# The first expert loop of a two-layer mixture kernel: results stored from two buffers, weights split by ScalarE and VectorE, loads issued by SyncE

## What is computed

```python
# first mixture: top 2 of 8 experts, width 256 -> 256 -> 256
inter = jnp.einsum('ecd,efd->ecf', binned, w1_stack)
inter = jnp.square(jax.nn.relu(inter))
outb = jnp.einsum('ecf,edf->ecd', inter, w2_stack)
moe_out = zeros.at[sorted_tok].add(outb[sorted_e, local_pos] * sorted_w[:, None])
...
# second mixture: top 2 of 8, width 256 -> 512 -> 256, with biases
h = jax.nn.silu(g) * u          # g = x @ gate_w + gate_b, u = x @ up_w + up_b
expert_out = jnp.einsum('nef,efd->ned', h, down_w) + down_b
y = jnp.einsum('ne,ned->nd', probs, expert_out)
```

## Time and profile before

| | us |
|---|---|
| median of 3 runs | 1300.96 |
| profiled execution, device time | 1300.48 |
| its span | 1298.7 |
| TensorE busy | 1114.3 (86%) |
| VectorE busy | 724.2 (56%) |
| ScalarE busy | 383.7 (30%) |
| GpSimd busy | 376.0 (29%) |

### The profile page before, as it was taken

How to read it: one execution, slowest core, us unless ns; L and a number is a source line. 1 busy time by engine, 2 the same in 40 slices (tenths; PEclk the granted TensorE clock), 3 DMA queues, 4 the chain that set the end, 5 groups by cost and what they waited for, 6 DMA issues and landing times.

```text
span 1298.7 us, 17826 instructions
## 1 busy us (share of the span) xinstructions
PE 1114.3 (86%) x5947; PEld 886.8 (68%) x5947; DVE 724.2 (56%) x1840; ACT 383.7 (30%) x705; POOL 376.0 (29%) x312
## 2 busy tenths in 40 slices
PE   8899899897766657999999967999999649999991
PEld 5467576685556554677887835787878339999990
DVE  5576735757444435465646554445354746666665
ACT  3131221312233224234243333243332123333330
POOL 2423062231435540001111123010101465444710
PEclk9999999999888889999999989999999969999995
DMA  9000051000475734100000000000000586555416
GB/s 327 1 0 34 1 185 28 1 1 5 141 203 161 227 109 137 33 1 1 1 1 1 1 34 34 1 1 1 1 1 1 176 269 186 153 155 168 128 55 210
DMA packets 90851, 102.92 MB, mean 79 GB/s; under 512 B 18336, under 2 KB 75936, under 8 KB 90656
## 3 DMA queue, kind: packets, MB, share of 16 engines
q1 hardware_dynamic: 65920, 59.85, 15.1%
q0 software_dynamic: 20240, 36.72, 9.1%
q10 hardware_dynamic: 4624, 5.51, 1.2%
HBM read 73.31 MB, written 28.74 MB: 79 GB/s over the span
## 4 chain that ended last, share of the span: by engine, by line
PE 50%; issue 18%; DVE 14%; DMA 7%; ACT 4%; POOL 4%; SPq 2%; DVEq 0%; POOLq 0%; ACTq 0%
PE PS L210 12%; PE PS L212 11%; PE PS L211 10%; PE PS L1709 7%; DMA results<-y,place_of 3%; PE PS L1597 2%; POOL routed L843 2%; PE PS L1569 2%; PE PS L1481 1%; PE PS L1681 1%; DMA split<-down_w 1%; POOL rstd L836 1%; DMA places<-routed 1%; PE PS L1475 1%; DVE hs L588 1%
## 5 line engine op out<-in xcount | busy, mean ns | idle before, releaser
L836 POOL TENSOR_TENSOR rstd<-ve,minus_half 128x4 f32<-128x4 f32 x40 | 41.3, 1033 | 350.9 <-DVE ve L1101 210.9
L535 POOL DMA_INDIRECT results<-y,place_of x80 | 78.2, 978 | 184.2 <-DVE y L624 110.5
L1481 PE MATMUL PS<-ones_bf 128*128 128x512 bf16 x393 | 103.7, 410 | 19.1 <-DMA routed<-S,dest 16.0
L210 PE MATMUL PS<-xt,split 128*128 128x256 f32 x312 | 90.2, 289 | 9.2 <-issue 6.1
L211 PE MATMUL PS<-xt,split 128*128 128x256 f32 x312 | 89.0, 285 | 0.0
L212 PE MATMUL PS<-xt,split 128*128 128x256 f32 x312 | 88.9, 285 | 0.0
L1709 PE MATMUL PS<-VP,HB 128*128 128x257 f32 x384 | 85.8, 382 | 0.7 <-DVE VP L1407 0.5
L843 POOL DMA_INDIRECT routed<-S,dest x64 | 66.1, 1033 | 67.1 <-DVE dest L1181 49.3
L1481 PEld LDWEIGHTS PS<-ones_bf 128*128 128x128 bf16 x393 | 39.0, 105 | 66.7 <-issue 34.2
L210 PE MATMUL PS<-split,hs 128*128 128x256 f32 x184 | 59.7, 324 | 25.8 <-DVE hs L588 19.9
L1709 PEld LDWEIGHTS PS<-VP,HB 128*128 128x128 f32 x384 | 72.5, 190 | 13.5 <-DVE VP L1407 3.4
(11 more groups left out here) (338 smaller groups left out, 2955.0 us busy)
## 6 DMA issues: line engine op xcount, KB each, us to landing
xg<-routed SPq DMA_DIRECT2D x42, 256.0 KB
HB<-results SPq DMA_DIRECT2D x16, 512.0 KB, 5.6
routed<-blank SPq DMA_DIRECT2D x20, 264.0 KB
raw<-gate_w SPq DMA_DIRECT2D x8, 512.0 KB
raw<-up_w SPq DMA_DIRECT2D x8, 512.0 KB
raw<-down_w SPq DMA_DIRECT2D x8, 512.0 KB
split<-m_w POOLq DMA_DIRECT2D x12, 256.0 KB, 3.2
split<-gate_w POOLq DMA_DIRECT2D x6, 512.0 KB
```

What stands on the lines that cost most here:

```text
L210: pe.matmul(out_, a[1], b[0], start=first, stop=False)
L535: pool.indirect_dma_start(out=results[m], out_offset=bass.IndirectOffsetOnAxis(ap=place_of[:, a:a + 1], axis=0), in_=w.y[:, a], in_offset= ...
L836: pool.tensor_tensor(rstd[h][:], ve[h][:], minus_half[:], ALU.pow).then_inc(sem(name), 1)
L1481: pe.matmul(free.rearrange("p (a b) -> p a b", b=P), ones_bf[:], ones_bf[:].unsqueeze(1).to_broadcast([P, TT, P]), start=True, stop=True)
```

## The change

Row and tags of a token are loaded by one DMA; VectorE copies the tags on (`tag`). There are two result buffers `y` and two `place_of`, used in turn. In the first loop ScalarE copies both halves of the results out of PSUM in one instruction, and GpSimd only stores. The hi weights of the first loop are made by ScalarE (for expert e+2 at the start of expert e), the lo weights by VectorE (for e+1); SyncE issues the raw loads, with three buffers, and the next layer's weights. Three things outside the loop move too: `y_free` goes to GpSimd's start, with four writes for the first mixture; the load of `DB` goes behind `first_group_in`; and in front of the first loop SyncE issues the write of `x_base` for the third sequence and a weight load ahead of `first_group_in`.

```diff
-            w.xg = sb(f"xg{m}", [P, G // P, D], F32, st)
+            w.xg = S2T[0][:, 0:G // P]
-            w.y = sb(f"y{m}", [P, G // P, D], F32, st)
+            w.y = S1[1][:].rearrange("p (i a) d -> p i a d", i=2)
...
         def group_in(sp, m, t):
-                sp.wait_ge(sem(f"m{m}_turned"), t)
+                sp.wait_ge(sem(f"m{m}_tagged"), t)
-            sp.dma_start(into, routed[m][bass.ds(r, G), 0:D].rearrange("(a p) d -> p a d", p=P)).then_inc(sem(name), 16)
-            sp.dma_start(places[:, bass.ds(t * (G // P), G // P)], routed[m][bass.ds(r, G), D:D + E].rearrange("(a p) e -> p a e", p=P))\
-              .then_inc(sem(f"m{m}_places"), 16)
+            sp.dma_start(into, routed[m][bass.ds(r, G), :].rearrange("(a p) d -> p a d", p=P)).then_inc(sem(name), 16)
...
         def moe_sp(sp, m):
-                if m == 1 and e + 2 < E:
-                    raw_in(sp, m, e + 2)
-                if m == 0 and e == 5:
+                if e + 3 - m < E:
+                    raw_in(sp, m, e + 3 - m)
+                if m == 0 and 2 <= e < 7:
+                    attention_weights(sp, e - 2)
+                elif m == 0 and e == 7:
...
+        def weights_hi(act, m, e):
+            raw_there(act, m, e)
+            act.activation(moe[m].split[e % 3][0], raw_of(m, e), ACT.Copy).then_inc(sem(f"m{m}_hi"), 1)
...
         def y_free(pool, m):
             for a in range(G // P):
-                pool.dma_start(results[m][2 * B * T + a:...], blank[0:1, a, 0:D]).then_inc(sem(f"m{m}_yout{a}"), 16)
+                for k in range(1 if m else 1 + 2 * a):
+                    if k:
+                        pool.wait_ge(sem(f"m{m}_yout{a}"), 16 * k)
+                    pool.dma_start(results[m][2 * B * T + 2 * k + a:...], blank[0:1, a, 0:D]).then_inc(sem(f"m{m}_yout{a}"), 16)
...
+        def moe_pool_first(pool):
+            def group_out(t, i):
+                pool.wait_ge(sem("m0_y"), t + 2)
+                for a in range(G // P):
+                    rows_out(pool, 0, i, a, f"m0_yout{i}")
...
         def moe_act(act, m):
                 if m == 0 and e + 2 < E:
-                    raw_in(act, 0, e + 2)
+                    weights_hi(act, 0, e + 2)
...
                     x_hi(t + 2)
+                    else:
+                        act.wait_ge(sem("m0_placed"), t + 1)
+                        act.wait_ge(sem("m0_down"), t + 1)
+                        act.activation(w.y[:, bass.ds(t % 2, 1)]..., PS[:, 5:7, 0:D], ACT.Copy).then_inc(sem("m0_y"), 1)
...
         def moe_dve(dve, m):
+            tag(1)
             x_lo(1)
+            if m == 1:
+                dve.wait_ge(sem("cw_raw"), 96)
             for e in range(E):
+                if m == 0 and 2 <= e + 1 < E:
+                    weights_lo(dve, 0, e + 1)
...
+                        if f == w.fc - 1:
+                            tag(t + 2)
                         if f:
                             h_lo(t, f - 1)
...
+                    if m == 0:
+                        dve.wait_ge(sem("m0_yout0"), 32 * (t // 2) + 16)
+                        dve.wait_ge(sem("m0_yout1"), 32 * ((t + 1) // 2) + 16)
+                        dve.tensor_copy(place_of[:, bass.ds(t % 2, 1)], tags[:, bass.ds(t % 2, 1), :, e]).then_inc(sem("m0_placed"), 1)
...
@@ block.sync
-                    if n == PAIRS * 2 - 2:
-                        first_group_in(sp, 0)
                     sp.wait_ge(sem("batch_a"), n + 1)
                     sp.dma_start(x_base[0, n]..., X[h][:]).then_inc(sem(f"x_out{h}"), 16)
+                    if n == PAIRS * 2 - 2:
+                        raw_in(sp, 0, 2)
+                        first_group_in(sp, 0)
...
-            sp.dma_start(DB[:], down_b...).then_inc(sem("db_in"), 16)
             first_group_in(sp, 1)
+            sp.dma_start(DB[:], down_b...).then_inc(sem("cw_raw"), 16)
...
@@ block.gpsimd
             pool.wait_ge(sem("pool_c"), 11)
+            pool.wait_ge(sem("blank"), 2)
+            for m in two:
+                y_free(pool, m)
             ln = [0]
```

More of the change, by code:

```diff
@@ L145, in build @@
         carry = sb("carry", [P, TT + 1, E])
[L146 to L147 removed]
+        tags = sb("tags", [P, 2, G // P, E])
+        place_of = sb("place_of", [P, 2, G // P], I32)
         table = [sb(f"table{m}", [1, 64], I32) for m in range(2)]
@@ L468, in first_group_in, with all_groups @@
                 sp.wait_ge(sem(f"scattered{h}"), 16 * 2 * TT * PAIRS * (m + 1))
-            group_in(sp, m, 0)
-            group_in(sp, m, 1)
+            for i in two:
+                group_in(sp, m, i)
             for e in range(3, E):
                 fill(sp, m, e, "filled")
+        def all_groups(eng, m):
+            return eng.value_load(table[m][0:1, 2 * E - 1:2 * E], min_val=E, max_val=NG)
         def moe_sp(sp, m):
@@ L487, in moe_sp, with weights_cast @@
             moe_end(sp, m, hi)
[L489 to L496, removed]
+        def weights_cast(pool, m, e):
+            if m == 1 and e >= 3:
+                done = pool.value_load(table[1][0:1, e - 2:e - 1], min_val=1, max_val=NG - 1)
+                counted(pool, 1)
+                pool.wait_ge(sem("m1_down"), done)
+            name = "m0_cast" if m == 0 else f"m1_cast{e % 2}"
@@ L507, in weights_lo @@
+            hi, lo = moe[m].split[e % 3]
             eng.tensor_tensor(lo, raw_of(m, e), hi.bitcast(F32), ALU.subtract).then_inc(sem(f"m{m}_lo"), 1)
-        def attention_weights_hi(pool):
-            for dst, src in ((WHH, whh),):
-                pool.dma_start(dst[:, 0], src.rearrange("(c p) o -> p c o", p=P)).then_inc(sem("cw_hi"), 16)
         def y_free(pool, m):
             for a in range(G // P):
-                pool.dma_start(results[m][2 * B * T + a:2 * B * T + a + 1], blank[0:1, a, 0:D]).then_inc(sem(f"m{m}_yout{a}"), 16)
@@ new lines, in moe_pool_first @@
+        def moe_pool_first(pool):
+            pool.wait_ge(sem("m0_table"), 1)
+            total = all_groups(pool, 0)
+            def group_out(t, i):
+                counted(pool, 0)
+                pool.wait_ge(sem("m0_y"), t + 2)
+                pool.sem_inc(sem("passed"), 1)
+                for a in range(G // P):
+                    rows_out(pool, 0, i, a, f"m0_yout{i}")
+            with pool.Fori(0, total // 2) as k:
+                for i in two:
+                    group_out(2 * k + i, i)
+            group_out(total - 1, 0)
+            moe_end(pool, 0, total)
@@ L577, in moe_dve, with tag @@
             w = moe[m]
+            def tag(n):
+                dve.wait_ge(sem(f"m{m}_turned"), n)
+                rows = first_rows if isinstance(n, int) else w.xg
+                dve.tensor_copy(tags[:, bass.ds((n - 1) % 2, 1)], rows[:, :, D:D + E].unsqueeze(1)).then_inc(sem(f"m{m}_tagged"), 1)
             def x_lo(n):
@@ L915, in _ @@
                     power(h)
-                    if n == B - 1:
-                        pool.wait_ge(sem("batch_c"), B)
-                        for e in range(2):
-                            weights_hi(pool, 1, e)
                 elif stage == "scatter":
@@ L999, in _ @@
             moe_act(act, 0)
+            act.wait_ge(sem("cw_raw"), 80)
+            act.activation(WHH[:, 0], raw_whh, ACT.Copy).then_inc(sem("cw_hi"), 1)
             after(act, "gt_ps")
@@ L1072, in _ @@
                     route_exp(1, n, h)
+            for e in range(2):
+                weights_hi(act, 1, e)
             act.wait_ge(sem("m1_table"), 1)
```

124 lines of the change are left out of this document (61 added, 63 removed).

## The result

The changed kernel took 1337.16 us, the median of four runs (1336.43 to 1339.84), against 1300.60 for the kernel before on the same chip: ratio 1.0291, 95% interval 1.0276 to 1.0306. The forecast was 1297.9, and its range ended at 1309.

A forecast was written before the change was run, and what follows sets the result against it. TensorE waits a third of the first loop, behind VectorE's 33.9 us of buffer and tag waits. −20.1 − 1 + 3 + 5.5 + 7.5 + 2 = −3.1 gives 1297.9 us; 8-in-10 range 1286 to 1309.

The forecast's parts named there:

- Term E: Second loop: the tag copy ahead of the third quarter's lo part costs 0.1 us in each of 21 rounds, +2 us (0 to 5).
- Term C: Kernel's start: six one-row writes, two waiting for a landing, delay GpSimd's first power, +5.5 us (1.4 to 8.2).
- Term D: Second loop's start: the bias table, issued behind the five fills, holds VectorE's first round, +7.5 us (5 to 12).
- Term B: Before the first loop: SyncE's fills wait for the third sequence's sum and queue behind other transfers, +3 us (−1 to +7).
- Term A: First loop, groups 2 to 18: double buffers remove VectorE's waits, rounds fall to 4.7 us, −20.1 us (−25.7 to −8.7).
- the tail: First loop's end, behind the last rows copy: the last group's own wait goes, −1 us.
- The fourth rival: First loop: VectorE's new lo weights hold up GpSimd's stores, 1.2 us at six experts, 1305.1 us in all; chance 0.05.
- The second rival: First loop: the single row buffer becomes the bound, rounds 5.6 us with landings of 4.6, 1308.7 us in all; chance 0.20.

The follow-up runs named there:

- the experiment: A program of GpSimd and VectorE alone, no kernel: small VectorE instructions of twelve forms, each run alone and beside a long GpSimd instruction; 16-number SBUF copy 0.17 us or 5.82.
- the fills first: Changed kernel with SyncE issuing the first loop's fills and first rows before it waits for the third sequence's sum: 1338.27 us, ratio 1.0297 to the kernel before.
- the copy on ScalarE: Changed kernel with the second loop's tag copy made by ScalarE, behind the last hi part of a round: 1296.01 us, ratio 0.9994 to the kernel before.
- the table first: Changed kernel with the bias table loaded before the second loop's fills and first rows again: 1323.28 us, ratio 1.0212 to the kernel before.

## Why the prediction was wrong, step by step

**Term E failed**, and with it the result: "The tag copy stands before the lo part of the third quarter ... 21 × 0.1 = +2; ends 0 and, at 0.25 each, 5." It was +37.7. I had seen that there is no slack at this place, and priced the copy by how long such a copy lasts alone. My upper bound, 0.41 us, came from the result copy of the earlier trace rows, which reads PSUM, a form that GpSimd doesn't hold up (0.17 in the experiment). I didn't ask what GpSimd does at that moment. One row of the trace before would have calmed me, VectorE's cast of a tag in the middle of the subtraction:

```profile
1086.47 6.88 POOL L507 TENSOR_TENSOR third_split<-raw,third_split 128x3072 fp32r<-128x3072 f32 x1
...
1091.33 0.15 DVE L620 CAST place_of<-places 128x1 int32 x1 [1.39 <-PE PS L212]
```

It casts one number, the form that the experiment shows to be free. The new copy has 16. Other rows of the same trace give the warning that I missed, GpSimd, then VectorE:

```profile
198.23 2.40 POOL L507 TENSOR_TENSOR split<-raw,split 128x1024 fp32r<-128x1024 f32 x1 [7.44 <-DMA split<-m_w]
200.60 5.24 POOL L864 TENSOR_TENSOR EMB<-EMB,rowv 128x1024 f32<-128x1024 f32 x2
...
199.48 1.16 DVE L1254 TENSOR_TENSOR kb<-kb,colv 128x2 f32<-128x2 f32 x1
200.68 2.29 DVE L1256 TENSOR_TENSOR kb<-colv,kb 128x2 f32<-128x2 f32 x1
```

Two instructions on two numbers with two SBUF inputs, 0.16 us each elsewhere in the trace, last 1.16 and 2.29 us; the first ends at 200.64, GpSimd's subtraction at 200.63. The copy alone in the kernel before (1.0306) and its absence (0.9994) show the step from both sides. Of the 37.7 us the copies stand 25, and 11 are the longer busy time of TensorE at the lower clock.

With term E as forecast the time would have been some 1302.6, inside the range: all other stages together came to −0.4 us, forecast −5.1. That is partly luck. C and D were 9.3 us too low and B 2.1; A, the tail and the stages taken as nothing were 6.6 too high.

**The fourth rival had the pair and the wrong direction.** It let VectorE hold up GpSimd's stores (3.61 us beside 3.34), and weighed only the new lo weights of the first loop. The same rows read the other way, who came first keeps the other out, would have led to GpSimd's subtractions of 6.9 us in the second loop, one just before it and six in its rounds, and to every new SBUF copy beside them. What I named for it, the Trainium skill ("GPSIMD Engine Reference", Key points), speaks of contention and gives no direction; I took one.

**Term C** was a sum of 1.4 to 8.2 with 5.5 taken; the writes cost 7.8, inside, near the upper row as argued. The other 3.3 carry the term, 11.1, beyond its range, and are again GpSimd and VectorE: the late power put the band selects beside the normalisations. I had the power on the path of everything that follows, and didn't ask what that would then meet.

**Term D**, +7.5 of 5 to 12: +11.2 in the trace, 10.3 by the run without it. Right in kind, taken too low. I expected the table at 1070.6 or 11.2 us behind the rows copy of 1059.42; it held VectorE until 15.9 us behind its own. The issue came when forecast, 4.7 us behind the rows copy (forecast 4.4). Mis-sized was the landing: I took 6.8 us from the start of the issue, and VectorE went on 11.1 after it, near the 11.3 of the earlier trace rows that I had as the upper end.

**Term B**, +3 of −1 to +7: +5.1. The order was as described, VectorE's sum waited for "remote" again (8.26 us) and the fills followed it:

```profile
355.74 1.28 DVE L1371 SCALAR_TENSOR_TENSOR X<-PS,tanh_g,X 128x1024 f32<-128x1024 f32 x1 [8.26 <-remote]
357.05 0.37 SPq L820 DMA_DIRECT2D x_base<-X  x1
357.46 1.53 SPq L438 DMA_DIRECT2D S<-m_w  x2
360.25 2.69 SPq L466 DMA_DIRECT2D routed<-blank  x3
```

What I left out is that "the fills first" would not have helped: the cast that waits for the third expert's weights stands in ScalarE's queue ahead of the first round. I priced that cast at its 1.06 us and not at its wait.

**Term A held**: −24.3, with −20.1 forecast and −25.7 as the lower end. Rounds were 4.5 us (forecast 4.7), since in this loop, with no GpSimd arithmetic beside it, the tag copy lasts 0.2 to 0.4 us; 0.9 at an expert's start (1.1). The second rival, row loads as the bound, was wrong: TensorE waited 7.8 us for rows in the whole loop, 5.5 of them at its start.

So the first loop's part of the change is a gain of 22 us, ratio 0.983, and what buried it are 38.6 us of a copy in the other loop, 10.3 of a table and 8.5 to 11 of six one-row writes.

**Open.** What "remote" is, which holds VectorE's sum (and TensorE's shared products, by up to 4.0 us in all) before the first loop, isn't settled. Of twelve traces nine have it, 6.3 to 8.3 us long. The three without it are the copy in the kernel before, the copy on ScalarE and the table first, where the sum waited 1.5 to 3.2 us for TensorE; they ran on one chip, on which the kernel before took 1296.53 instead of 1299.5 to 1300.6. So it seems to go with the chip and not with the kernel, and ratios within a chip should bear it little. A part of term B stands without it: on that chip the stretch from the scatter to the rows copy of group 2 is 46.8 us in the order before and 49.6 and 51.2 in the new one, 2.8 to 4.4 more, against 5.1 where the idle time is. In the same way the rounds of the second loop, 236.8 us in the changed kernel and 199.8 with the copy on ScalarE, give 37.0 without any such share.

## What to carry to other kernels

An instruction added to VectorE is not priced by its own length but by what GpSimd runs at that moment: from SBUF to SBUF, with more than one number or with two SBUF inputs, it can last as long as GpSimd's instruction, so it belongs on ScalarE, on an operand in PSUM, or where nobody waits behind it. Such instructions can be looked for in the trace before the change: the same form, a few of them many times as long as the rest, each ending with one of GpSimd's. When something is moved to an engine's start, list what then runs beside what, not only how late it all becomes. And a copy or cast that waits for a load stalls every later instruction of its engine: look at what it waits for before its price.

## What the runs showed of the hardware that I had not expected

- The shared path holds for the whole instruction: a 16-number copy of 0.17 us took 5.82 beside a subtraction of 6.65, 0.99 beside a select of 1.89 and 1.74 beside a memset of 2.66, each to its end within 0.05 us.
- Two SBUF inputs wait for a select (0.98) and not for a memset (0.17).
- A DMA of a single row of 1 KB was waited for 5.44 and 4.38 us behind its issue at the kernel's start, with 381 GB/s in the queues, and 1.33 us where they were all but empty.
